# Scale gathers of a 4-bit gate/up layer taken in pairs of tiles and moved ahead, with the order of a few neighbours changed

## The reference, cut to what matters

```python
x = x + ffn0(cond0(x))
x = x + ffn1(cond1(x))
# ffn0
w_gu = scales_gu[g_idx] * (nibbles(qweight_gu) - (nibbles(qzeros_gu)[g_idx] + 1))   # [512, 2*1376]
gate, up = split(x @ w_gu)
w_d = scales_down[g_idx_d] * (nibbles(qweight_down) - (nibbles(qzeros_down)[g_idx_d] + 1))
return (silu(gate) * up) @ w_d
```

## Time and profile before

| what | value |
|---|---|
| time, median of 3 runs | 461.98 us (460.03 to 462.97) |
| time of the profiled execution | 461.01 us |
| its span, first to last instruction | 459.2 us |
| mean granted TensorE clock | 0.996 |
| busy: TensorE | 444.0 us (97%) |
| busy: VectorE | 343.7 us (75%) |
| busy: ScalarE | 218.9 us (48%) |
| busy: GpSimd | 216.9 us (47%) |

### The profile page before, as it was taken

The page is one execution under the profiler, slowest core; times in us unless marked ns, Lnnn a source line. Parts: engine busy times, 40 slices in busy tenths (PEclk is TensorE's granted clock), DMA queues, the critical chain, the costliest instruction groups (busy, mean ns, idle before and its releaser), DMA issues.

```text
span 459.2 us, 5528 instructions
## 1 busy us (share of the span) xinstructions
PE 444.0 (97%) x1946; PEld 358.4 (78%) x1946; DVE 343.7 (75%) x439; ACT 218.9 (48%) x283; POOL 216.9 (47%) x187
## 2 busy tenths in 40 slices
PE   8998899989999996999999999999999999999997
PEld 4686788867778885888888778888888888888885
DVE  3867898877685888966596857867868678999922
ACT  4413755444564011525557766646466455374200
POOL 2177898888845500630002769797896700000000
PEclk9999999999999998999999999999999999999999
DMA  7753111111115868076448824857948346795633
GB/s 270 190 183 99 53 44 46 49 46 47 46 46 171 263 244 316 0 309 212 168 148 317 332 101 144 263 160 243 283 151 256 121 160 243 283 333 173 202 118 137
DMA packets 30807, 79.96 MB, mean 174 GB/s; under 512 B 2960, under 2 KB 16048, under 8 KB 29120
## 3 DMA queue, kind: packets, MB, share of 16 engines
q1 hardware_dynamic: 26608, 68.05, 43.1%
q0 software_dynamic: 3600, 10.84, 7.5%
q10 hardware_dynamic: 576, 0.79, 0.5%
HBM read 58.95 MB, written 20.72 MB: 173 GB/s over the span
## 4 chain that ended last, share of the span: by engine, by line
PE 71%; POOL 15%; issue 7%; DVE 4%; DMA 1%; ACT 1%; POOLq 0%; ACTq 0%; DVEq 0%
PE ps L1865 10%; PE ps L1867 10%; PE ps L1866 10%; POOL scale L620 8%; PE ps L1611 6%; PE ps L1612 6%; PE ps L1615 6%; PE ps L1968 5%; PE ps L1967 5%; PE ps L1969 5%; PE ps L1848 2%; PE ps L1846 2%; PE ps L1847 2%; POOL raw L648 2%; POOL raw L651 2%
## 5 line engine op out<-in xcount | busy, mean ns | idle before, releaser
L1611 PE MATMUL ps<-h_hi,ring_hi 128*128 128x512 f32 x152 | 60.0, 395 | 6.6 <-issue 3.5
L620 POOL DMA_INDIRECT scale<-in_sc_gu,idx_gu x44 | 59.9, 1361 | 12.3 <-issue 11.7
L1612 PE MATMUL ps<-h_lo,ring_hi 128*128 128x512 f32 x152 | 59.9, 394 | 0.0
L1067 DVE TENSOR_TENSOR ring_lo<-raw,ring_hi 128x1792 fp32r<-128x1792 f32 (+1 forms) x23 | 45.5, 1978 | 17.6 <-ACT ring_hi L704 17.4
L704 ACT ACTIVATE ring_hi<-raw 128x1792 fp32r<-128x1792 f32 (+1 forms) x23 | 36.6, 1592 | 41.1 <-POOL raw L651 15.8
L1865 PE MATMUL ps<-zt_hi,ring_hi 128*128 128x512 f32 x140 | 54.5, 390 | 0.4 <-issue 0.4
L1867 PE MATMUL ps<-zt_hi,ring_lo 128*128 128x512 f32 x140 | 54.5, 389 | 0.0
L1866 PE MATMUL ps<-zt_lo,ring_hi 128*128 128x512 f32 x140 | 54.5, 389 | 0.0
L1615 PE MATMUL ps<-h_hi,ring_lo 128*128 128x512 f32 x152 | 48.2, 392 | 0.0
L1611 PEld LDWEIGHTS ps<-h_hi,ring_hi 128*128 128x128 f32 x152 | 28.9, 190 | 13.4 <-issue 7.4
L1612 PEld LDWEIGHTS ps<-h_lo,ring_hi 128*128 128x128 f32 x152 | 29.0, 191 | 6.0
(11 more groups left out here) (250 smaller groups left out, 1119.6 us busy)
## 6 DMA issues: line engine op xcount, KB each, us to landing
ad_raw<-in_w1T SPq DMA_DIRECT2D x8, 1024.0 KB, 4.9
wd<-down_weights SPq DMA_DIRECT2D x7, 1024.0 KB, 5.7
down_weights<-dhi SPq DMA_DIRECT2D x7, 896.0 KB, 4.5
down_weights<-dlo SPq DMA_DIRECT2D x7, 896.0 KB, 4.1
raw<-in_gu SPq DMA_DIRECT2D x12, 512.0 KB, 3.7
wd<-down_weights SPq DMA_DIRECT2D x7, 768.0 KB, 4.8
draw<-in_d SPq DMA_DIRECT2D x7, 512.0 KB, 5.1
dn_work<-in_qw_dn SPq DMA_DIRECT2D x11, 256.0 KB, 3.3
```

What stands on the lines that cost most here:

```text
L620: pool.indirect_dma_start(dst, None, table, bass.IndirectOffsetOnAxis(ap=index, axis=0)).then_inc(done, 16)
L1067: dve.tensor_tensor(dst, src, hi_part.bitcast(F32), ALU.subtract).then_inc(done_sem, 1)
L1611: pe.matmul(ps[:, bank + hf, :], w_hi, v_hi[:, t], start=first, stop=False)
L1612: pe.matmul(ps[:, bank + hf, :], w_hi, v_lo[:, t], start=False, stop=False)
```

## The change

- Scales are stored for two tiles side by side (`sc_gu`: rows of 2 KB; the last, odd tile has its own table `sc_last` with 1 KB rows). `scales_gu(j)` fetches the pair (2j, 2j+1) with four gathers; j = 5 is the single last tile. 24 gathers instead of 44.
- The pairs lie in five places (at 108, 48, 108, 48, 56 KB) and the last at 64 KB, so that pair 4 and the last have places of their own; `y_raw` moves to 184 KB. The arrival is counted on three semaphores.
- GpSimd's order: scales 0, 1, `lnb`, scales 4, sums(2), scales 2, sums(3), scales 3, scales 5, then the sums of tiles 4 to 8.
- VectorE's order at the start: both early parts of the zeros, dequant 0 and 1, w_lo 0 and 1, the last part of the zeros, dequant 2, the four y_split, dequant 3.
- Down: table arrivals are counted in groups of (2, 2, 4, 3); x is reloaded after load_qd(8) instead of load_qd(4); w_hi_dn(1) stands ahead of h_split(10) on ScalarE, w_lo_dn(1) ahead of gate_times_up(10) and h_split(10) on VectorE.
- The reciprocal of the normalisation signals VectorE's own semaphore instead of `s_rc`.

```diff
-SC_KB = tuple((64, 112)[i % 2] if i != FT0 - 2 else 196 for i in range(FT0))
+NPAIRS = FT0 // 2
+TD_GROUPS = (2, 2, 4, 3)
...
-        scale = [region(kb, f"scale{i}", [P, 8 * P], F32) for i, kb in enumerate(SC_KB)]
+        scale = [region(kb, f"scale{j}", [P, KD, 4 * P], F32) for j, kb in enumerate((108, 48, 108, 48, 56))]
+        scale.append(region(64, "scale_last", [P, KD, 2 * P], F32))
...
-        y_raw = region(48, "y_raw", [P, KD, T], F32)
+        y_raw = region(184, "y_raw", [P, KD, T], F32)
...
+        s_sc = [sem(f"s_sc{c}") for c in range(3)]
+        SC_SEM = (0, 1, 0, 1, 2, 2)
+        SC_DONE = (1, 1, 2, 2, 2, 2)
...
-                if k == 4:
+                if k == 8:
                     sp.wait_ge(s_wf, FT0)
...
-            pool.dma_start(lnb[:, :], a["lnw"].partition_broadcast(P)).then_inc(s_ln, 16)
-
-            def scales_gu(i):
-
-                need(pool, s_wf, i - 1)
+            def scales_gu(j):
+
                 for k in range(KD):
-                    gather(scale[i][:, 256 * k:256 * k + 256], a["sc_gu"], idx_gu[:, i, k:k + 1], s_raw["gu0"][i % 2])
+                    table, index = (a["sc_gu"], idx_gu[:, j, k:k + 1]) if j < NPAIRS else (a["sc_last"], idx_gu[:, 0, k:k + 1])
+                    gather(scale[j][:, k, :], table, index, s_sc[SC_SEM[j]])
...
-            for i in range(4):
-                scales_gu(i)
-            for i in BLOCK_TILES:
+            def sums_gu(i):
                 pool.wait_ge(s_wf, i + 1)
                 sums(sum_at("q", i), *blocks0(i % 2))
-                if i + 2 < FT0:
-                    scales_gu(i + 2)
+
+            scales_gu(0)
+            scales_gu(1)
+            pool.dma_start(lnb[:, :], a["lnw"].partition_broadcast(P)).then_inc(s_ln, 16)
+            scales_gu(4)
+            sums_gu(2)
+            scales_gu(2)
+            sums_gu(3)
+            scales_gu(3)
+            scales_gu(5)
+            for i in BLOCK_TILES[2:]:
+                sums_gu(i)
...
             silu(FT0 - 1)
+            w_hi_dn(1)
             h_split(FT0 - 1)
-            w_hi_dn(1)
...
-                dve.wait_ge(s_raw["gu0"][s], (i - s) * 32 + 64)
-                dve.scalar_tensor_tensor(out=raw0[s][:, 0:8 * P], in0=nib[:, 2 * P * i:2 * P * i + 2 * P].bitcast(U8), scalar=16.0,
-                                         in1=scale[i][:, :], op0=ALU.subtract, op1=ALU.mult).then_inc(s_wf, 1)
+                j = i // 2
+                dve.wait_ge(s_sc[SC_SEM[j]], 16 * KD * SC_DONE[j])
+                dve.scalar_tensor_tensor(out=raw0[s][:, 0:8 * P].rearrange("p (k c) -> p k c", k=KD),
+                                         in0=nib[:, 2 * P * i:2 * P * i + 2 * P].bitcast(U8).rearrange("p (k c) -> p k c", k=KD),
+                                         scalar=16.0, in1=scale[j][:, :, 2 * P * s:2 * P * s + 2 * P],
+                                         op0=ALU.subtract, op1=ALU.mult).then_inc(s_wf, 1)
...
             add_zeros(0)
+            add_zeros(1)
             dequant_gu(0)
-            add_zeros(1)
+            dequant_gu(1)
             w_lo(0)
-            dequant_gu(1)
+            w_lo(1)
             add_zeros(2)
-            w_lo(1)
+            dequant_gu(2)
             y_split(0, 0)
             y_split(1, 4)
-            dequant_gu(2)
             y_split(2, 6)
             y_split(3, 2)
+            dequant_gu(3)
...
+            w_lo_dn(1)
             gate_times_up(FT0 - 1)
             h_split(FT0 - 1)
-            w_lo_dn(1)
```

More of the change, by code:

```diff
@@ L274, in build @@
         s_idx, s_zg, s_aok = (sem(n) for n in ("s_idx", "s_zg", "s_aok"))
-        s_td = [sem(f"s_td{c}") for c in range(len(D0_CHUNK))]
+        s_td = [sem(f"s_td{c}") for c in range(len(TD_GROUPS))]
+        s_sc = [sem(f"s_sc{c}") for c in range(3)]
+        SC_SEM = (0, 1, 0, 1, 2, 2)
+        SC_DONE = (1, 1, 2, 2, 2, 2)
         s_warm = sem("s_warm")
         s_v = sem("s_v")
-        s_raw = {p: [sem(f"s_raw_{p}{s}") for s in range(2)] for p in ("gu0", "gu1")}
+        s_raw = {p: [sem(f"s_raw_{p}{s}") for s in range(2)] for p in ("gu1",)}
         s_qw = sem("s_qw")
@@ L292, in build @@
         s_xr = sem("s_xr")
-        s_rhi, s_rlo, s_sq, s_rt, s_rc, s_zs, s_zt = (
-            sem(n) for n in ("s_rhi", "s_rlo", "s_sq", "s_rt", "s_rc", "s_zs", "s_zt"))
+        s_rhi, s_rlo, s_sq, s_rt, s_zs, s_zt = (
+            sem(n) for n in ("s_rhi", "s_rlo", "s_sq", "s_rt", "s_zs", "s_zt"))
         s_ocp = sem("s_ocp")
@@ L411, in table_group @@
         def table_group(k):
-            return sum(k >= sum(D0_CHUNK[:c]) for c in range(1, len(D0_CHUNK)))
+            return sum(k >= sum(TD_GROUPS[:c]) for c in range(1, len(TD_GROUPS)))
         def d0_ring(ring, e):
@@ L1198, in dequant_gu @@
                 need(dve, s_wlo, i - 1)
-                dve.wait_ge(s_raw["gu0"][s], (i - s) * 32 + 64)
-                dve.scalar_tensor_tensor(out=raw0[s][:, 0:8 * P], in0=nib[:, 2 * P * i:2 * P * i + 2 * P].bitcast(U8), scalar=16.0,
-                                         in1=scale[i][:, :], op0=ALU.subtract, op1=ALU.mult).then_inc(s_wf, 1)
+                j = i // 2
[4 more added lines that the diff above has]
+                                         op0=ALU.subtract, op1=ALU.mult).then_inc(s_wf, 1)
             def dequant_dn(k):
-                dve.wait_ge(s_td[table_group(k)], 16 * D0_CHUNK[table_group(k)])
+                dve.wait_ge(s_td[table_group(k)], 16 * TD_GROUPS[table_group(k)])
                 dve.wait_ge(s_qd[k % 3], 16 * (k // 3 + 1))
@@ L1292, in _ @@
             w_lo(2)
-            dequant_gu(3)
             y_sum_lo(3)
@@ L1373, in norm @@
                 rstd = col[:, 2 * NBATCH + b:2 * NBATCH + b + 1]
-                dve.reciprocal(rstd, col[:, NBATCH + b:NBATCH + b + 1]).then_inc(s_rc, 1)
-                dve.wait_ge(s_rc, b + 1)
+                own(dve.reciprocal(rstd, col[:, NBATCH + b:NBATCH + b + 1]))
                 dve.scalar_tensor_tensor(out=zn[:, b % 4, :], in0=ps[:, z_bank(b), :], scalar=rstd, in1=lnb[:, :],
@@ L2040 @@
     sg = pad_f(v["L0_ffn_scales_gu"]).reshape(G_GU, 2, FT0, P)
+    sc_rows = sg.transpose(2, 0, 1, 3).reshape(FT0, G_GU, 2 * P)
     qd = np.repeat(v["L0_ffn_qweight_down"], 8, axis=0)
@@ L2061 @@
         "qw_gu": np.ascontiguousarray(qg.transpose(0, 2, 1, 3)).view(np.uint8).reshape(64, FT0, 2 * P, 4).transpose(0, 1, 3, 2).reshape(64, -1).view(np.uint32),
-        "sc_gu": sg.transpose(2, 0, 1, 3).reshape(FT0 * G_GU, 256),
+        "sc_gu": sc_rows[:2 * NPAIRS].reshape(NPAIRS, 2, G_GU, 2 * P).transpose(0, 2, 1, 3).reshape(NPAIRS * G_GU, 4 * P),
+        "sc_last": sc_rows[2 * NPAIRS],
         "qz_gu": pad_f(v["L0_ffn_qzeros_gu"]).reshape(16 * G_GU, -1),
```

## The result

The changed kernel takes 448.66 us, the median of four executions (447.99 to 451.79). The kernel before took 461.87 beside it, also in four. The ratio is 0.9731, with a 95% interval of 0.9674 to 0.9788. The forecast was 450.0 in a range from 446.5 to 456.0. The profiled execution took 448.04 us, with a span of 446.3 and a granted clock of 1.000; before, it was 461.01, 459.2 and 0.996.

A forecast was written before the change was run, and what follows sets the result against it. TensorE, busy 97% of the span, was taken as the bound, so gains are its closed pauses. 1.5 + 5.9 + 3.5 + 1.7 - 0.5 = 12.1 us off 461.98 gave 449.9, written as 450.0, range 446.5 to 456.0.

The forecast's parts named there:

- Block tiles: Tiles 3 to 8: with gathers moved out, GpSimd no longer delays them and the 9.52 us period holds; gain 5.9 us.
- The stall at tile 3: Eight gathers ahead of sums(4) may make TensorE wait at tile 3: charged 0.5 us, between none and some 3.5.
- The start: Ahead of the first gate matmul: paired scales let VectorE reach y_split(0) earlier, so gate(0) begins 1.5 us earlier.
- The first down: Unit 1 of the first down: its 3.5 us pause closes, and the clock does not fall behind it, another 1.7 us.
- the 1.5 at unit 2: First down, unit 2: its low part ready by 184.6 at the latest, wanted at 186.1, so 1.5 us in hand.
- Any two of them would do: First down: any two of (a), (b) and the earlier w_hi_dn(1) and w_lo_dn(1) (2.4 us) close the pause.
- (a): First down: table groups of two let VectorE's first dequant_dn start at 147.9 instead of 150.42; 2.5 us.
- (b): First down: the wait for a weight load queued behind 2 MB of x goes; 1.4 us.
- 1 (the start gives nothing): Start: 2 KB rows land late, or zeros and dequant(2) ahead of y_split eat the gain; 451.5 us, chance 0.14.
- 2 (the pause moves to unit 2): First down: pause and clock loss stay or move to unit 2; 455.2 us, chance 0.12.
- 3 (long gathers): Block tiles: eight gathers of 2.34 us each hold sums(4) back, stalling tile 3 by 5.6 to 9 us; 458.5, chance 0.08.
- 4: GpSimd: gathers cost by their bytes, so 2 KB rows take 3.3 us and the kernel slows; 482.9 us, chance 0.04.

The follow-up runs named there:

- Experiment 1: The kernel before with only the first down's edits (table groups, x reload after load 8, w_hi_dn(1) and w_lo_dn(1) moved ahead): 456.09 us, 0.9908 of before.
- Experiment 4: The changed kernel with VectorE's old order at the start, so dequant(3) comes later, behind w_lo(2): 455.68 us, 0.9888 of before.
- experiment 3: The changed kernel with 44 gathers of one tile's 1 KB rows instead of 24, in the same places and order: 475.05 us, 1.032 of before.
- experiment 8: The changed kernel with dequant(2) behind y_split 0 and 1, last tile's gathers behind sums(4), and the first pair's four gathers ahead of the zeros': 455.41 us.
- 5: The changed kernel with h_split(10) again ahead of w_hi_dn(1) and w_lo_dn(1): 450.88 us, 0.9779 of before.
- 6: The changed kernel with unit 1's old order and table groups (4, 4, 3), x still reloaded behind load 8: 452.62 us, 0.9841 of before.
- 2: The changed kernel with all of the first down's edits undone: 454.59 us, 0.986 of before.
- 8 to 10: First pair's gathers ahead of the zeros': all four in experiment 8 (455.41 us), four in the changed kernel (455.95), two in experiment 8's base (450.22).

## Why the prediction was right

- **Block tiles, 5.9 us**: 5.89 measured, with the mechanism as told. ScalarE and VectorE do carry the 9.52 us period once GpSimd has no gathers between the sums. Experiment 1 bears out that GpSimd set the pace of this stage before: there tile 8 came no later although the start had lost time.
- **The stall at tile 3, -0.5 us**: none came. The forecast had y_snap_5 end at 82.8 for a due time of 82.9; it ended at 82.3 for a due time some 0.4 later. Here luck helped. GpSimd's last sum of tile 4 ended at 80.0 where 80.5 was forecast, but by errors that cancel: sums(2) began 1.7 us early (46.33) and pair 2 took 7.7 us instead of 9.4, while sums(3) took 5.9 instead of 3.3. The charge was a guess between 0 and 3.5, and its reason was wrong: the first two of the eight gathers did not run beside an idle VectorE and took 1.76 and 1.97 us; the idle time came later, beside the middle four. Experiment 4 shows how close the other end is: with dequant(3) later it is 4.5 us.
- **The start, 1.5 us**: 1.8 less idle time, 1.2 in the span of this execution. The landing of 2 KB rows was put at 3.9 us; six traces in which VectorE waited for it give 3.2 to 4.3, with a mean of 3.6. The price that the Trainium skill (DMA: Bandwidth & Descriptors, Anatomy of one DMA) puts on the doubling, 0.3 us on the 2.9 of the earlier trace rows, makes 3.2, the shortest of the six. VectorE's chain was put at 7.4 us and took 7.5 (36.50 to 43.97). What the forecast missed is that both ends of this chain move between executions by 2 us and more, and the clock with them. Its 1.5 was compared with one early execution; over the traces the gain is 0.5 in the mean. This term is the least secure of the sum.
- **The first down, 3.5 + 1.7 us**: 4.0 and about 1.8. VectorE's low part came within 0.2 us of the forecast (172.3, less the 7.1 us by which tile 8 came earlier, for 165.35). The 2.9 us in hand at unit 1 were 2.3, since TensorE came 0.5 earlier than forecast; the 1.5 at unit 2 were 1.0 (low part done at 177.46 for 178.50). "Any two of them would do" was tested for one pair, (a) and (b), and holds with 0.1 us to spare. With (b) alone the pause came back at 1.62 us.
- **The rivals.** 1 (the start gives nothing) did not happen in the first profile, but the traces together do not exclude it: its 1.5 us are within the scatter of the start. 2 (the pause moves to unit 2) did not happen; 3 (long gathers) did not either, as two of the eight were near 2 us or above and the others 0.94 to 1.76; 4 was refuted by the groups (1352 ns) and by experiment 3. In this run of eight the four of 1.43 to 2.49 us lay beside VectorE's work on two SBUF operands, as the Trainium skill (SBUF — State Buffer, Who interferes with whom) has it, and the four of 0.94 or 0.95 us beside an idle VectorE or one that read PSUM. But not every gather beside such work is long: the one at 38.85 took 0.94 us beside a w_lo. Eight long ones would have needed such work throughout, and VectorE had none from 67.47 to 72.12.
- **The sum** was 12.1 for 12.9 measured. The 0.8 are the stall that did not come (0.5), the way to unit 1 (0.5) and what lies behind it (0.1), less the start (0.3). In medians the change was 13.2 us in the first comparison and 10.5 in the second, and the executions of the changed kernel lie 4 us apart (447.99 to 451.96). That the sum comes so near in one profile is in part luck.

## What to carry to other kernels

Where an engine pays by the instruction and not by the byte, let one gather serve two users, and spend the room on issuing ahead of the stretch that is short of that engine. Such a burst only works if what stands ahead of it is early, so look at the producer (here dequant(3)) before judging the burst. A pause in front of the bound engine costs more than its length if the clock falls behind it, so shortening one that varies is worth more than its mean length. Before moving a DMA issue into a wait that looks free, try it: here moving the whole pair cost 6 to 8 us, at an instruction of VectorE that uses nothing of what was gathered. And time lost or won ahead of a stretch that another engine holds back can vanish in it, as in experiment 1.

## What the runs showed of the hardware that was not expected

- GpSimd's share of an indirect gather does not depend on the row: 1361 ns in the mean for 1 KB rows and 1352 for 2 KB, 973 for the 2.8 KB rows of the zeros, and 0.95 us for nearly every one, of 2 and of 2.8 KB, that ran while VectorE stood still (experiment 8).
- A pause of TensorE of 1.8 to 3.2 us was sometimes followed by a stretch at the lower clock level (0.50 of 2.4 GHz, so 1.2) of 3.4 us and sometimes not: 3.15 us without and with (experiment 1), 2.12 with (5), 2.02 without (6), 1.80 with (3). The pauses of 3.40 us and more in these traces were all followed by it. It lasted 3.4 us behind the 3.40 of the changed kernel's second profile and the 3.48 of the earlier trace rows, and 6.8 us in the five traces with pauses of 3.85 to 5.07 (2, 4 and 8 to 10). That spread alone is some 1.7 us between executions of one kernel.
- VectorE stood still for 9 to 11 us, with all its waits in the program fulfilled, in the three traces in which GpSimd's first gathers began 2 to 4 us earlier (8 to 10). Why is open.
